# Routing inside the edge stage of a graph attention and mixture-of-experts kernel: one scan for the counts, two pieces for the ranks, the one-hots of the lists on ScalarE

## The reference

```
x = x + gnn(layernorm(x), W, a_src, a_dst, src, dst)
x = x + ffn(layernorm(x), ...)

gnn: z = h @ W per head (4 heads of 64)
     e = leaky_relu(es[src] + ed[dst]);  alpha = softmax of e over the edges of one dst
     out = segment_sum(alpha * z[src], dst)
ffn: logits = x @ gate_w + gate_b;  the 2 best of 16 experts, softmax of their logits
     h = relu(x @ w1[e] + b1[e]);  y = h @ w2[e] + b2[e];  moe = the weighted sum of the two
     layernorm(x + moe) * gamma + beta
```

## Time and profile before

| | us |
|---|---|
| median of 3 runs | 2656.95 |
| the profiled execution | 2657.41 |
| its span, first to last instruction | 2655.6 |
| PE busy in it | 1843.6 |
| DVE busy | 1833.8 |
| POOL busy | 1791.7 |
| ACT busy | 773.5 |

### The profile page before, as it was taken

The page is one execution under the profiler, slowest core; times in us unless marked ns, Lnnn a source line. Parts: engine busy times, 40 slices in busy tenths (PEclk is TensorE's granted clock), DMA queues, the critical chain, the costliest instruction groups (busy, mean ns, idle before and its releaser), DMA issues. The chain is left out here.

```text
span 2655.6 us, 58129 instructions
## 1 busy us (share of the span) xinstructions
PE 1843.6 (69%) x9114; PEld 1441.3 (54%) x9115; DVE 1833.8 (69%) x5880; ACT 773.5 (29%) x3120; POOL 1791.7 (67%) x1935
## 2 busy tenths in 40 slices
PE   7566666666666666666666666666666669999977
PEld 5344444444544444445445444555454459999975
DVE  6577777777777767777777778888877756633326
ACT  4433212212121211122122212121212235555547
POOL 0577777777777777777777776777777725555547
PEclk9688888877878888788788877888798879999999
DMA  9544555545554544455455544544445446665437
GB/s 313 148 134 133 138 131 144 141 134 138 142 137 137 140 138 138 136 138 142 134 136 144 137 133 116 136 133 129 128 133 139 128 139 212 212 200 171 154 123 243
DMA packets 199437, 397.10 MB, mean 150 GB/s; under 512 B 40565, under 2 KB 99360, under 8 KB 198730
## 3 DMA queue, kind: packets, MB, share of 16 engines
q0 software_dynamic: 87264, 241.69, 33.4%
q1 hardware_dynamic: 88952, 131.34, 15.9%
q10 hardware_dynamic: 22898, 20.85, 2.8%
HBM read 358.45 MB, written 33.93 MB: 148 GB/s over the span
## 5 line engine op out<-in xcount | busy, mean ns | idle before, releaser
L815 POOL DMA_INDIRECT ring<-z_table,src_idx x1602 | 1523.2, 951 | 526.3 <-issue 469.5
L1221 PE MATMUL psMb<-msg,S 128*128 128x260 f32 x3608 | 1192.5, 487 | 458.0 <-DVE msg L1069 457.7
L1221 PEld LDWEIGHTS psMb<-msg,S 128*128 128x128 f32 x3608 | 819.8, 238 | 639.6 <-DVE msg L1069 494.7
L1069 DVE TENSOR_TENSOR msg<-ring,psPb 128x1024 f32<-128x1024 f32 x451 | 546.8, 1212 | 0.0
L1118 ACT COPY es_edge<-ring 128x16 f32 x451 | 91.5, 203 | 1338.4 <-SPq L743 1290.0
L887 DVE TENSOR_TENSOR earg<-es_edge,dest_sum 128x16 f32<-128x16 f32 x451 | 80.2, 178 | 333.5 <-ACT es_edge L1118 290.1
L875 DVE TENSOR_TENSOR S<-iota_f,psPb 128x512 f32<-128x512 f32 x451 | 306.5, 680 | 1.2 <-ACT psPb L1127 1.1
L1187 PEld LDWEIGHTS psEb<-node_thirds,ST 128*128 128x128 bf16 x1804 | 104.4, 105 | 298.5 <-issue 275.7
L869 DVE TENSOR_SCALAR ST<-dst_bc,iota_p 128x512 bf16 x451 | 170.2, 377 | 128.8 <-issue 123.7
L1344 POOL DMA_INDIRECT rows_sb<-norm_rows,src_sb x108 | 105.3, 975 | 192.5 <-DVE src_sb L1464 121.6
L1187 PE MATMUL psEb<-node_thirds,ST 128*128 x1804 | 120.5, 179 | 163.3 <-DVE earg L904 91.8
(11 more groups left out here) (298 smaller groups left out, 1673.0 us busy)
## 6 DMA issues: line engine op xcount, KB each, us to landing
dst_bc<-dst_rows SPq DMA_DIRECT2D x202, 256.0 KB, 3.5
w_all<-in_L_ffn_w_dram SPq DMA_DIRECT2D x64, 512.0 KB
ring<-z_table,src_idx POOLq DMA_INDIRECT x1602
side<-z_table SPq DMA_DIRECT2D x1280, 1.0 KB
b_sb<-in_L_ffn_b_dram ACTq DMA_DIRECT2D x108, 128.0 KB
got<-pair_rows SPq DMA_DIRECT2D x48, 256.0 KB, 4.1
z_table<-z_out SPq DMA_DIRECT2D x49, 130.0 KB, 6.5
norm_rows<-xnb ACTq DMA_DIRECT2D x49, 128.0 KB
```

The costliest lines, as they stand in the source:

```text
L815: nc.gpsimd.indirect_dma_start(ring[:, s, c, :], None, z_table, bass.IndirectOffsetOnAxis(ap=at, axis=0)).then_inc(b_landed[s], 16)
L1069: nc.vector.tensor_tensor(msg[:, s % MR, :, 0:D].rearrange("p g (h d) -> p g h d", h=HEADS), ring[:, bass.ds(slot, 1), :, 0:D].rearrange(" ...
L1221: last = nc.tensor.matmul(psM[s % 2][:, 0:ROW], S[:, s % MR, c, :], msg[:, s % MR, c, :], start=c == 0, stop=c == G - 1)
```

## The change

Three parts in stage (b), and two in the tables.

1. *Waiting.* `a_step` goes. Each routing operation on DVE now waits, ahead of itself, for the one before it (`in_turn`), and nothing waits behind it.
2. *Counts, small steps and ranks.* `taken_a` and `cum_a` are laid out with the expert outside and the tile inside. One scan over all 480 columns takes the place of the thirty additions; it runs on over the experts, so `upto` holds the running sums and two more small operations take off what came before. The small steps are spread two to an iteration (330 to 341). The ranks come in two pieces of 15 tiles (240 columns), four iterations each (341 to 348), with at most three operations in one.
3. *Lists.* They start at 351 instead of 355. ACT makes the one-hots, as Relu(1 - (column - value)^2): Square and Relu for the low one, and Square and Relu with a scale and a bias for the high one, which is to hold a value instead of 1. There are three buffers instead of two, and DVE and PE take a list four iterations on (LISTED = 4), counted as in the code, instead of two.
4. In stage (a), `val_neg`, one more operation of 60 columns.
5. The tables of the visits lie in one tensor at partitions 0, 32 and 64, and each engine loads its registers from there.

```diff
-        CUM, PIECE_TILES = 3, 6
+        PIECE_TILES = 15
...
-        CUM_END = AT + NA // CUM
-        ON_SMALL = CUM_END + 3
-        ON_PAST = ON_SMALL + 3
+        ON_SMALL = AT + 4
+        ON_PAST = ON_SMALL + 10
         ON_PIECE = ON_PAST + 1
-        ON_RUN = ON_PIECE + 2 * PIECES
+        ON_RUN = ON_PIECE + 4 * PIECES
         ON_LISTS = ON_RUN + 2
-        ON_TABLE = ON_LISTS + TOP * NA + 2
+        LISTED = 4
+        ON_TABLE = ON_LISTS + TOP * NA + LISTED
...
+        visit_tables = sb(graph, "visit_tables", [65, VISITS], I32)
+        visit_tile, group_free, visit_group = visit_tables[0:1, :], visit_tables[32:33, 0:GROUPS + 1], visit_tables[64:65, :]
...
+                        step(nc.vector.tensor_scalar(val_neg[:, :, :], val_i[:, :, 0:NA], -1.0, None, ALU.mult))
...
-                    def a_step(instruction):
+                    def in_turn():
+                        if early_steps[0]:
+                            dve.wait_ge(b_astep, early_steps[0])
                         early_steps[0] += 1
-                        instruction.then_inc(b_astep, 1)
-                        dve.wait_ge(b_astep, early_steps[0])
...
-                        if AT < i <= AT + NA // CUM:
-                            for t in range(CUM * (i - AT - 1), CUM * (i - AT)):
-                                a_step(nc.vector.tensor_tensor(cum_a[:, t + 1, :], cum_a[:, t, :], taken_a[:, t, :], ALU.add))
+                        if i == AT + 1:
+                            in_turn()
+                            nc.vector.tensor_tensor_scan(cum_a[:, 1:], over(ones[:, 0:1], [P, EXPERTS * NA]), taken_a[:, :, :].rearrange("p e t -> p (e t)"),
+                                                         0.0, ALU.mult, ALU.add).then_inc(b_astep, 1)
...
+                            if i == ON_PIECE + 4 * n + 1:
+                                in_turn()
+                                nc.vector.tensor_tensor(ranked, ranked, beyond, ALU.add).then_inc(b_astep, 1)
+                                in_turn()
+                                nc.vector.tensor_tensor(beyond, ranked, hot[:, 0, at, :].rearrange("p t e -> p e t"), ALU.mult).then_inc(b_astep, 1)
...
-                        if 0 <= i - ON_LISTS < TOP * NA:
-                            u = i - ON_LISTS
-                            t, k = divmod(u, TOP)
-                            nc.vector.tensor_scalar(low_a[:, u % 2, :], iota_f[:, :], parts_a[:, LO, k, t:t + 1], None, ALU.is_equal)
-                            nc.vector.tensor_scalar(high_a[:, u % 2, :], iota_f[:, 0:CA + EXPERTS], parts_a[:, HI, k, t:t + 1], val[:, k, t:t + 1],
-                                                    ALU.is_equal, ALU.mult).then_inc(b_ahot, 1)
...
+                        if 0 < i - LISTED - ON_LISTS < TOP * NA:
+                            in_turn()
+                            nc.vector.tensor_tensor(listed[:, :], listed[:, :], beside[:, 0:CA + EXPERTS], ALU.add).then_inc(b_astep, 1)
...
+                    def ahead(i):
+                        u = i - 3 - ON_LISTS
+                        if not 0 <= u < TOP * NA:
+                            return
+                        t, k = divmod(u, TOP)
+                        if u == 0:
+                            act.wait_ge(b_astep, A_LIST)
+                        if u >= 3:
+                            act.wait_ge(b_sum, ON_LISTS + u - 3 + LISTED - SUMMED + 2)
+                        low, high = low_a[:, u % 3, :], high_a[:, u % 3, :]
+                        nc.scalar.activation(low, iota_f[:, :], ACT.Square, bias=parts_a[:, LO, k, t:t + 1])
+                        nc.scalar.activation(high, iota_f[:, 0:CA + EXPERTS], ACT.Square, bias=parts_a[:, HI, k, t:t + 1]).then_inc(b_asquare, 1)
+                        act.wait_ge(b_asquare, u + 1)
+                        nc.scalar.activation(low, low, ACT.Relu, bias=ones[:, 0:1], scale=-1.0)
+                        nc.scalar.activation(high, high, ACT.Relu, bias=val[:, k, t:t + 1], scale=val_neg[:, k, t:t + 1]).then_inc(b_ahot, 1)
-                    written_out(VISITS, SR, [(open_group, AHEAD + 2), (locate, AHEAD + 3), (exponent, AHEAD + 3), (finish, None)], steps=FINISH)
+                    written_out(VISITS, SR, [(open_group, AHEAD + 2), (locate, AHEAD + 3), (exponent, AHEAD + 3), (finish, None), (ahead, None)], steps=FINISH)
...
                             pe.wait_ge(b_ahot, u + 1)
-                            nc.tensor.matmul(beside[:, 0:CA + EXPERTS], low_a[:, u % 2, :], high_a[:, u % 2, :], start=True, stop=True)
+                            pe.wait_ge(b_ahot, u + 1)
+                            nc.tensor.matmul(beside[:, 0:CA + EXPERTS], low_a[:, u % 3, :], high_a[:, u % 3, :], start=True, stop=True)
```

More of the change, by code:

```diff
@@ L708, in gnn_moe_kernel @@
             xnT = sb(ctx, "xnTb", [P, XN, D])
[L709 to L710 removed]
+            taken_a = sb(ctx, "taken_a", [P, EXPERTS, NA], BF16)
+            cum_a = sb(ctx, "cum_a", [P, 1 + EXPERTS * NA], BF16)
+            upto = sb(ctx, "upto", [P, 1 + EXPERTS])
+            before_a, through_a = (cum_a[:, lo:lo + EXPERTS * NA].rearrange("p (e t) -> p e t", e=EXPERTS) for lo in range(2))
             small_i = sb(ctx, "small_i", [P, 2, EXPERTS], I32)
[L712 removed]
+            own_a = sb(ctx, "own_a", [P, 2, EXPERTS, PIECE_TILES])
             slot_ai = sb(ctx, "slot_ai", [P, 2, TOP, NA], I32)
[L714 to L715 removed]
+            low_a = sb(ctx, "low_a", [P, 3, P])
+            high_a = sb(ctx, "high_a", [P, 3, CA + EXPERTS])
             parts_a = sb(ctx, "parts_a", [P, 2, TOP, NA])
@@ L1012, in ahead @@
                             at = slice(n * PIECE_TILES, (n + 1) * PIECE_TILES)
-                            if i == ON_PIECE + 2 * n:
-                                a_step(nc.vector.tensor_tensor(own_a[:, 1, :, :], own_a[:, 1, :, :], over(small[:, BEYOND, :].unsqueeze(1), wide), ALU.mult))
-                                a_step(nc.vector.tensor_tensor(own_a[:, 0, :, :], own_a[:, 0, :, :], own_a[:, 1, :, :], ALU.add))
-                            if i == ON_PIECE + 2 * n + 1:
-                                for k in range(TOP):
-                                    a_step(nc.vector.tensor_tensor(own_a[:, 1, :, :], own_a[:, 0, :, :], hot[:, k, at, :], ALU.mult))
-                                    a_step(nc.vector.tensor_reduce(slot_a[:, k, at], own_a[:, 1, :, :], AX.X, ALU.add))
@@ L1035, in ahead @@
                             assert early_steps[0] == A_STEPS
                     def take_aside(i, beside):
-                        wide = [P, PIECE_TILES, EXPERTS]
+                        wide = [P, EXPERTS, PIECE_TILES]
                         if i == ON_SMALL:
                             assert early_steps[0] == A_CUM
-                            a_step(nc.vector.tensor_copy(small[:, LEFT, :], beside[:, 0:EXPERTS]))
-                        if ON_PIECE <= i < ON_RUN and (i - ON_PIECE) % 2 == 0:
-                            rank = beside[:, 0:PIECE_TILES * EXPERTS].rearrange("p (t e) -> p t e", e=EXPERTS)
-                            a_step(nc.vector.tensor_tensor(own_a[:, 1, :, :], rank, over(small[:, LIMIT, :].unsqueeze(1), wide), ALU.is_ge))
-                            a_step(nc.vector.tensor_tensor(own_a[:, 0, :, :], rank, over(small[:, BASE, :].unsqueeze(1), wide), ALU.add))
@@ new lines, in take_aside @@
+                        if ON_PIECE <= i < ON_RUN and (i - ON_PIECE) % 4 == 0:
+                            rank = beside[:, 0:PIECE_TILES * EXPERTS].rearrange("p (e t) -> p e t", e=EXPERTS)
+                            in_turn()
+                            nc.vector.tensor_tensor(own_a[:, 1, :, :], rank, over(small[:, LIMIT, :].unsqueeze(2), wide), ALU.is_ge).then_inc(b_astep, 1)
+                            in_turn()
+                            nc.vector.tensor_tensor(own_a[:, 0, :, :], rank, over(small[:, BASE, :].unsqueeze(2), wide), ALU.add).then_inc(b_astep, 1)
```

213 lines of the change are left out of this document (132 added, 81 removed).

## The result

The changed kernel takes 2632.95 us (median of 4 runs, 2631.61 to 2634.52), the kernel before 2656.3 us (median of 4). The ratio is 0.9911 with a 95% interval of 0.9894 to 0.9928: faster by 23.4 us. The profiled execution took 2631.61 us for a span of 2629.8 us.

A forecast was written before the change was run, and what follows sets the result against it. POOL's gather issue paces the edge stage; only 27.6 us held by DVE could be won. 14.2 - 0.5 (lists) + 11 (counts, ranks) - 0.2 (rest) = 24.5 us; against the median 2632.5 us, range 2627 to 2646.

The forecast's parts named there:

- The two terms: Gains in POOL's held time: 14.2 - 0.5 us in the list stretch, 11 us in counts and ranks.
- What bounds the kernel: Edge stage: POOL paces at 1.254 us per gather; only the 27.6 us in which DVE held it can be won.
- The lists: List stretch: a DVE visit falls from 4.34 to 3.60 us, winning all but 0.5 of 14.2 us.
- a lack of 0.11 us per visit: List stretch: DVE's visit of 4.34 us was under POOL's 4.45 us by only 0.11 us.
- ACT: List visits: four activations take 1.5 us, bringing ACT to 2.4 us in 4.45 us; costed at nothing.
- Rival 1: List stretch: ACT's four activations delay the score copy as much as DVE was relieved; 2646 us, chance 0.10.
- The slower rival: List visits: Exp's table lacks Square, so ACT loads a table twice a visit; 2677 us, chance 0.04.
- Counts and small steps: Routing stretch: scan 1.2 us once, about 4.7 us in two visits; small steps about 4.1 us a visit.
- Ranks: Routing stretch: sixteen operations of 0.40 us, 6.5 to 7 us in eight visits, about 4.55 us a visit.
- What would show it: Routing stretch back at about 340 gathers per 430 us; DVE's wait for ACT's scores 35 us or more.
- Two signs: 1540 to 1970 us: POOL's message wait under 12 us; some 2 us of its wait remaining beside a batch.
- the some 2 us that were to remain: Rank visits where a batch is finished: 5.9 us made against about 4 us in hand leaves POOL waiting.

The follow-up runs named there:

- the first experiment: The kernel before with only the lists' one-hots moved to ACT (three buffers, taken four iterations on, tables stacked), waits still behind: 2644.59 us, ratio 0.9957.

## Why the prediction was right, and where it was not

The time, 2632.5 us forecast and 2632.95 measured, came from a sum of 24.5 us against 23.4, so from the right ceiling. The two terms came as well: between the same gathers 13.0 us in the lists (13.7 forecast) and 10.6 in counts and ranks (11). What the experiments take apart is which of the edits earned them.

**What bounds the kernel.** Right. POOL's pace of 1.254 us per gather did not move, and only the 27.6 us in which it was held could be won. The version with the one-hots on DVE has 21.5 us more of DVE in the list stretch and the same time: a DVE cheaper than needed won nothing more, as the prediction said. The granted clock of TensorE does not explain the gathers: in the routing stretch it was 0.77 with 99 of them and 0.83 with 98, in the two kernels with those waits ahead. Two readings of the prediction were loose and changed nothing: POOL's row has one slice at 6 tenths inside the edge stage, the 25th (1593 to 1660 us), which lies in the routing stretch, and the list stretch held 62 visits (220 / 3.552), not 65.

**The lists.** The size held (10 of 11.3 gathers, 12.5 us, against 13.7), and the visit of 3.60 us was measured at 3.64, 3.56 at the tenth percentile. What failed is the credit: "The change takes the two one-hots off DVE (0.43 us) and lets the accumulation follow the addition at once" was priced as one edit that had to bring 0.74 us. The margin needed was far less. The wait alone makes the visit 3.98 us, 0.47 us under POOL's pace, and brings 9 gathers; ACT alone, with the wait behind, brings 5; with both, ACT adds one (277.0 against 278.9 us between the same gathers), which the time does not show. The prediction had both prices (0.43 and 0.38 us) beside a lack of 0.11 us per visit and did not ask what either alone would do.

**ACT.** The activations took 1.57 us a list added up, 1.41 from end to end, forecast 1.5. By the rule of the Trainium skill ("ScalarE: Activation LUTs", Rules for kernel authors) relu belongs on VectorE. Here the trace agrees on the durations, 1.41 us of ACT against 0.43 of DVE, and yet the times are the same (0.9911 against 0.9908), as either engine had the time. Rival 1 did not come in the changed kernel, but its place was right: the first experiment and the kernel with four more activations both held POOL longest where a batch is scaled and where the activations stand between group and score. With ACT busy 4.85 us a visit (270.23 x 3.552 / 198) instead of 1.95 (126.42 x 3.552 / 230), ACT did come between group and score: its wait for groups in the list stretch, 128.6 us in the changed kernel, is gone, DVE waits 77.4 us there for ACT's scores and POOL 47.9 us for the message.

**The slower rival.** No table is loaded more: ten loads for Exp in the edge stage, ten for the root, three elsewhere, in both kernels. So Square ran with the table of Exp and with that of the root. Its price was about right all the same: the kernel with twelve more activations has 198 gathers in 290 us, 5.2 us a visit (290 x 3.552 / 198), for which the prediction worked out 2677 us; it took 2671.84, and 28.5 us more in the lists than the kernel before, where 31 were worked out. ACT as the bound came from work added there, not from table loads.

**Counts and small steps.** Right: 1.15 us for the scan against 1.2, 4.09 us a visit against 4.1. Both held.

**Ranks.** Right in the sum, wrong in the operation. Of the eight, two multiplications took 0.59 us and two sums 0.55 us instead of 0.40; sixteen make 2 x (0.42 + 0.40 + 0.59 + 0.55 + 0.59 + 0.54 + 0.40 + 0.41) = 7.8 us instead of 6.5 to 7. The extra of 0.8 to 1.3 us was the price of the turned reads (four operations of a piece took 0.12 to 0.19 us more than the other four), well under the 4.5 us that the prediction allowed for. A rank visit without a batch beside it took 4.40 to 4.64 us, forecast 4.55. What the prediction left out is that the wait's place was worth as much as the rewriting: with the old counts and ranks, the wait alone brought 5 gathers, the rewriting alone 4 (93 to 97), both 9. It had the mechanism, "DVE's queue cannot run ahead over a wait", for the counts, and it put the lost lead into the visits of the changed kernel (4.1 and 4.55 us), but it never asked what the old ranks would gain from the wait's place.

**What would show it.** POOL has 339 gathers in 1540 to 1970 us, as forecast; DVE waits 57.2 us for the scores, over 35. Two signs missed by a little: POOL's wait for the message is 14.8 us where under 12 was named, and the some 2 us that were to remain are 5.2 in the whole stretch.

**The wait.** It is the term that the prediction undervalued, and the rows show two parts of it. The kernel before with its waits ahead has nothing else changed, so that the wait's place is shown to be the cause of its gain; how the gain splits into the two parts was not measured. One is the gap: from the start of the addition to listed to the start of the accumulation 0.51 us with the wait (1753.19 to 1753.70), 0.16 without (1701.88 to 1702.04). The other I read as DVE's lead over its own queue: from a destination sum to the addition behind it there are 0.35 us in a bare visit and 0.71 us at the least in the ranks of the kernel before; in the same kernel with its waits ahead the smallest is 0.53 us, and 0.35 again in the ranks of the changed kernel. The Trainium skill ("VectorE: DVE Perf Modes", The DRAIN you can't avoid) says of eight copies in a row that a semaphore after each costs nothing extra over one after the last, and its Rules for kernel authors advise for chained operations to minimize their count, not the semaphores. Carried over to this kernel, that would have its waits moved ahead gain nothing. It gained 17 us: the instruction behind the wait here did not need what was waited for, and without the wait it started before the addition's end (0.16 us after the start of one of 0.23 us).

## What to carry to other kernels

Find first how much less the held engine must be held, per visit, and then the cheapest edit that gives that much: here 0.11 us a visit were lacking, and moving a wait from behind an instruction to ahead of its first reader won 17 of 23 us with no operation moved. Once the pacing engine is full, further relief of the others is worth nothing, and a second engine loaded for it becomes a risk in the few visits where it has other work (here the scaling of a batch). To price a wait on the own engine, look at what stands behind it in the queue, not at the wait's row.

## What the runs showed that was not expected

- A sum or a product of 240 fp32 columns read with a stride of 15 or 16 columns took 0.54 to 0.59 us, the other operations of 240 columns 0.40 to 0.42 us; an addition of 480 bf16 columns took 1020 ns turned, and 408 ns straight in the kernel before.
- Profiled executions whose work is the same up to there differ by some us early in the edge stage: the 739th gather starts between 1007.8 and 1013.4 us in twelve of the thirteen kernels and at 1015.5 us in the one whose profiled execution took 2658.39 us. From 1110 to 1540 us all have 341 to 344 gathers. Counts by fixed windows so carry an error of a few gathers; no cause was looked for.
